# State space layer: scan inputs multiplied on GpSimd, one scan over both batches

## What is computed

```
xp = xi @ W_x
delta = softplus(xp[..., :1] @ W_dt.T + b_dt)
Bp = xp[..., 1:d_state + 1]
Cp = xp[..., d_state + 1:]
A = -exp(A_log)
def step(h, inp):
    x_t, dt, Bt, Ct = inp
    A_bar = exp(dt[..., None] * A)
    h = A_bar * h + dt[..., None] * Bt[:, None, :] * x_t[..., None]
    y_t = einsum('bds,bs->bd', h, Ct) + D * x_t
    return (h, y_t)
```

## Time and profile before

| what | value |
|---|---|
| median of 3 runs | 2915.17 us (2914.5 to 2917.82) |
| the profiled execution's own time | 2910.92 us |
| its span in the trace | 2909.1 us |
| PE busy | 2417.7 us, 83% |
| DVE busy | 1550.1 us, 53% |
| ACT busy | 1058.6 us, 36% |
| POOL busy | 284.9 us, 10% |
| the stage of the 64 units, from the first u to the last hc | 2028.3 to 2188.4 us |

### The profile page before, as it was taken

The page is one execution under the profiler, slowest core; times in us unless marked ns, Lnnn a source line. Parts: engine busy times, 40 slices in busy tenths (PEclk is TensorE's granted clock), DMA queues, the critical chain, the costliest instruction groups (busy, mean ns, idle before and its releaser), DMA issues. The chain is left out here.

```text
span 2909.1 us, 39020 instructions
## 1 busy us (share of the span) xinstructions
PE 2417.7 (83%) x15028; PEld 1411.4 (49%) x15032; DVE 1550.1 (53%) x2487; ACT 1058.6 (36%) x1954; POOL 284.9 (10%) x589
## 2 busy tenths in 40 slices
PE   2899999688996959999983996785787979788778
PEld 1344444345895634444441554251225837555447
DVE  3778777232221638888845874234996533232433
ACT  2466666321111315777751552122221223021310
POOL 0453000010000000000000550000000000010100
PEclk8899999887998978999996567886877989898879
DMA  8887553110553896555400000101002341110200
GB/s 218 195 189 165 95 94 51 46 46 6 217 229 145 270 238 126 123 95 120 69 12 28 12 1 31 51 1 56 4 0 87 116 193 54 51 41 0 95 1 8
DMA packets 108646, 260.20 MB, mean 89 GB/s; under 512 B 11942, under 2 KB 83302, under 8 KB 94310
## 3 DMA queue, kind: packets, MB, share of 16 engines
q1 hardware_dynamic: 103276, 210.17, 28.4%
q0 software_dynamic: 1584, 34.60, 3.0%
q10 hardware_dynamic: 3600, 12.91, 1.1%
HBM read 212.72 MB, written 44.92 MB: 89 GB/s over the span
## 5 line engine op out<-in xcount | busy, mean ns | idle before, releaser
L664 DVE TENSOR_REDUCE sta_parts<-sta_psA 128x1 f32<-128x1024 f32 x544 | 625.6, 1187 | 193.9 <-PE sta_psA L580 192.1
L722 ACT ACTIVATE sta_probs<-sta_psS 128x512 f32<-128x512 f32 x1056 | 575.8, 597 | 274.4 <-PE sta_psS L591 272.3
L591 PE MATMUL sta_psS<-L_xattn_qS,L_xattn_kst 99*128 99x256 bf16 x2112 | 356.1, 278 | 11.5 <-ACT sta_probs L722 6.6
L580 PE MATMUL sta_psA<-L_xattn_kst,L_xattn_qS 99*128 99x512 bf16 x1088 | 293.7, 388 | 52.5 <-PEq L59 37.9
L591 PEld LDWEIGHTS sta_psS<-L_xattn_qS,L_xattn_kst 99*128 99x128 bf16 x2112 | 161.3, 98 | 259.1 <-ACT sta_probs L722 183.4
L601 PE MATMUL sta_psO<-sta_probs,L_xattna_V 128*32 128x256 f32 x2560 | 189.5, 385 | 0.0
L580 PEld LDWEIGHTS sta_psA<-L_xattn_kst,L_xattn_qS 99*128 99x128 bf16 x1088 | 104.3, 99 | 137.6 <-DVE sta_parts L664 45.9
L202 ACT ACT_TABLE_LOAD x14 | 18.0, 1283 | 334.8 <-PEq L59 316.6
L2274 PE MATMUL l2t_psY<-l2t_hc,top_consts_weights 128*128 128x512 f32 x128 | 92.5, 839 | 31.6 <-DVE l2t_hc L2310 31.5
L601 PE MATMUL sta_psO<-sta_probs,L_xattn_V 128*32 128x256 f32 x1536 | 114.3, 388 | 0.0
L1006 ACT ACTIVATE sht_probs<-sht_psS 128x768 f32<-128x768 f32 (+1 forms) x64 | 55.3, 863 | 149.4 <-PE sht_psS L850 100.3
(11 more groups left out here) (614 smaller groups left out, 4048.5 us busy)
## 6 DMA issues: line engine op xcount, KB each, us to landing
L_xattn_kst<-L_xattn_keys SPq DMA_DIRECT2D x192, 136.0 KB
L_xattn_kst<-L_xattn_keys SPq DMA_DIRECT2D x192, 128.0 KB
L_xattn_values<-prj_rows SPq DMA_DIRECT2D x64, 256.0 KB, 3.8
L_xattn_keys<-prj_parts SPq DMA_DIRECT2D x32, 384.0 KB, 3.9
L_xattna_V<-in_ctxV SPq DMA_DIRECT2D x5, 2048.0 KB, 11.7
L_xattna_V<-L_xattn_values SPq DMA_DIRECT2D x5, 2048.0 KB, 11.3
l2f_W<-in_M SPq DMA_DIRECT2D x10, 1024.0 KB, 7.5
L_xattn_keys<-sta_bparts SPq DMA_DIRECT2D x24, 384.0 KB, 7.2
```

What stands on the lines that cost most here:

```text
L580: last = nc.tensor.matmul(psA[:, u % 2, col:col + rhs.shape[1]], lhsT, rhs, start=True, stop=True)
L591: last = nc.tensor.matmul(psS[:, at % 2, j * T:(j + 1) * T], lhsT, rhs, start=True, stop=True)
L664: nc.vector.tensor_reduce(into(parts[:, u // n % 2]), view(psA[:, u % 2, :]), AX.X, ALU.max).then_inc(max_taken, 1)
L722: nc.scalar.activation(probs[:, u % NP, i * 512:(i + 1) * 512], psS[:, at % 2, :], ACT.Exp, scale=scale).then_inc(probs_ready, 1)
```

## The change

The products `u` move from DVE to POOL (L2308 of the changed kernel). ACT first copies psB of a state from PSUM into a new SBUF tile `rowsB` with two buffers (L2289); POOL multiplies rowsB with dx, both in SBUF, into `u`, now a ring of 3. DVE runs one scan over all 512 tokens for each unit (L2320) in place of two. So that the second batch starts from zero, column 0 and column 256 of `decay` stay at zero: DVE clears the ring once (L2313), and ACT writes only steps 1 to 255 of each batch (L2298), in one instruction of 2 x 255 elements. PE also waits, before it overwrites a psB buffer, for the copy of what was in it.

```diff
@@ -2244,11 +2244,18 @@
             psC = p2.ps("psC", [P, 2, 512])
             psY = p2.ps("psY", [P, CH, 512])
             decay = p2.sb("decay", [P, 3, NTOK])
-            u = p2.sb("u", [P, 2, NTOK])
+            u = p2.sb("u", [P, 3, NTOK])
             h = p2.sb("h", [P, 2, NTOK])
             hc = p2.sb("hc", [P, 3, NTOK])
-            with stage(nc, "spread", "input_ready", "decay_ready", "states_ready", "read_ready", "summed", "dve_step", "ahead_loaded") as \
-                    (block, spread, input_ready, decay_ready, states_ready, read_ready, summed, dve_step, ahead_loaded):
+            rowsB = p2.sb("rowsB", [P, 2, NTOK])
+            with stage(nc, "spread", "rows_copied", "starts_cleared", "input_ready", "decay_ready", "states_ready", "read_ready", "summed", "dve_step",
+                       "ahead_loaded") as \
+                    (block, spread, rows_copied, starts_cleared, input_ready, decay_ready, states_ready, read_ready, summed, dve_step, ahead_loaded):
+
+                def after_first(x):
+
+                    return x.rearrange("p (b t) -> p b t", b=B)[:, :, 1:T]
+
                 @block.sync
                 def _(sp):
                     load_ahead(sp, ahead, ahead_loaded)
@@ -2257,7 +2264,7 @@
                 def _(pe):
                     def spread_rows(s):
                         if s >= 2:
-
+                            pe.wait_ge(rows_copied, s - 1)
                             pe.wait_ge(read_ready, (s - 1) * CH)
                         n = 2 * NS + 1
                         for ps, r in ((psB, 1 + s), (psC, 1 + NS + s)):
@@ -2275,36 +2282,43 @@
 
                 @block.scalar
                 def _(act):
+                    def copy_rows(s):
+                        act.wait_ge(spread, s + 1)
+                        if s >= 2:
+                            act.wait_ge(input_ready, (s - 1) * CH)
+                        nc.scalar.copy(rowsB[:, s % 2, :], psB[:, s % 2, :]).then_inc(rows_copied, 1)
+
+                    copy_rows(0)
+                    act.wait_ge(starts_cleared, 1)
                     for i in range(NS * CH):
+                        if i % CH == 1 and i // CH + 1 < NS:
+                            copy_rows(i // CH + 1)
                         if i >= 3:
-                            act.wait_ge(states_ready, 2 * (i - 2))
-                        nc.scalar.activation(decay[:, i % 3, :], delta[:, i % CH, :], ACT.Exp, scale=A[:, i // CH:i // CH + 1]).then_inc(decay_ready, 1)
+                            act.wait_ge(states_ready, i - 2)
+                        nc.scalar.activation(after_first(decay[:, i % 3, :]), after_first(delta[:, i % CH, :]), ACT.Exp,
+                                             scale=A[:, i // CH:i // CH + 1]).then_inc(decay_ready, 1)
+
+                @block.gpsimd
+                def _(gp):
+                    for i in range(NS * CH):
+                        s, m = i // CH, i % CH
+                        gp.wait_ge(rows_copied, s + 1)
+                        if i >= 3:
+                            gp.wait_ge(states_ready, i - 2)
+                        nc.gpsimd.tensor_tensor(u[:, i % 3, :], rowsB[:, s % 2, :], dx[:, m, :], ALU.mult).then_inc(input_ready, 1)
 
                 @block.vector
                 def _(dve):
                     N = NS * CH
-
-                    def inputs(i):
-                        s, m = i // CH, i % CH
-                        dve.wait_ge(spread, s + 1)
-                        if i >= 2:
-
-                            dve.wait_ge(states_ready, 2 * (i - 1))
-                        nc.vector.tensor_tensor(u[:, i % 2, :], psB[:, s % 2, :], dx[:, m, :], ALU.mult).then_inc(input_ready, 1)
-
-                    inputs(0)
+                    nc.vector.memset(decay[:], 0.0).then_inc(starts_cleared, 1)
                     for i in range(N):
                         s, m = i // CH, i % CH
-                        if i + 1 < N:
-                            inputs(i + 1)
                         dve.wait_ge(decay_ready, i + 1)
                         dve.wait_ge(input_ready, i + 1)
                         if i >= 2:
                             dve.wait_ge(read_ready, i - 1)
-                        for b in range(B):
-                            c = slice(b * T, (b + 1) * T)
-                            nc.vector.tensor_tensor_scan(h[:, i % 2, c], decay[:, i % 3, c], u[:, i % 2, c], 0.0, ALU.mult, ALU.add).then_inc(states_ready, 1)
-                        dve.wait_ge(states_ready, 2 * (i + 1))
+                        nc.vector.tensor_tensor_scan(h[:, i % 2, :], decay[:, i % 3, :], u[:, i % 3, :], 0.0, ALU.mult, ALU.add).then_inc(states_ready, 1)
+                        dve.wait_ge(states_ready, i + 1)
                         if i >= 3:
                             dve.wait_ge(summed, i - 2)
                         nc.vector.tensor_tensor(hc[:, i % 3, :], psC[:, s % 2, :], h[:, i % 2, :], ALU.mult).then_inc(read_ready, 1)
```

## The result

The changed kernel takes 2945.11 us (median of 4 runs, 2943.23 to 2946.82) against 2915.0 for the kernel before (4 runs, 2914.5 to 2917.82): a ratio of 1.0101, 95% interval 1.0084 to 1.0119, slower by 30 us. The profiled execution took 2944.77 us, its span is 2942.9 us, against 2910.92 and 2909.1. POOL's time grew by the 85 us of its 64 products. The first scan starts at 2030.63 and the last hc at 2222.80, where the earlier trace rows had 2187.70: nearly all of the difference lies in the stage of the 64 units. PE's granted clock over that stage is 0.68, where the earlier trace rows had 0.77.

A forecast was written before the change was run, and what follows sets the result against it. DVE was taken to bound the stage, at 2.50 us a unit. Fourteen states at the expected clock mix, plus start and end, gave 139.5 + 44.8 - 140.0 = +44 us, so 2959 us; range 2925 to 2978.

The forecast's parts named there:

- DVE's own work: On DVE, u leaves and one scan replaces two: a unit with all inputs there takes 1.85 us, 0.65 less.
- The wait on ACT: On ACT, the next state's copy waits for PE's spread and holds back the exps and DVE's scans, in 14 states.
- X: Time from T to the start of scan 4s + 1: 4.38 us at PE's high clock, 7.12 at the low.
- The port: At SBUF, POOL's product goes first and DVE's scan waits: a contended unit takes 2.45 us, bounds 2.35 and 2.57.
- The fourth rival: At SBUF, POOL two products ahead takes its turn after the scan: 2.20 us a unit, +36 us; chance within the forecast's 0.67.
- The start and the end: Outside the 14 waiting states: scan 1 starts at 2032.9, and the last hc starts 7.91 us after the last T.
- First T: T is the end of unit 4s - 1's hc, from which a state is counted; the first was put at 2039.8.
- The clock: On PE, 10 of 14 spreads at the low clock (state 13.95 us), 4 at the high (11.21 us).
- Rival 1: No conflict between DVE's scan and POOL's product: 1.85 us a unit, +25 us with the expected clock mix; chance 0.20.
- rival 2: Conflict at SBUF, but PE stays at the high clock: +17 us; chance 0.10.
- rival 3: Faster: no conflict, high clock, and a spread reaching ACT sooner; a chain 0.5 us shorter gives -9 us; chance 0.03.
- signs named for a right forecast: DVE idle once a state, 1.9 or 4.7 us; scans 1.2 or 1.8; hc 0.69; stage 44 us longer; clock below 0.77.

The follow-up runs named there:

- either release of POOL: POOL's product i released by the scan of unit i - 3 or by its hc, in the changed kernel with its copy moved back: 2887.55 and 2889.95 us.
- the late copy: Changed kernel with ACT's copy of the next state's rows behind the exp of unit 4s + 3, not ahead of unit 4s + 1's: 2887.55 us.
- kernel with PE kept busy: Changed kernel with the products of units 4s + 1 and 4s + 2 made twice on PE, 32 more in all: 2945.58 us.
- pair with added products: Kernel before plus 64 POOL products into a tile nobody reads, released by the unit's scans or by its hc: 2911.98 and 2956.52 us.
- two different kernels: Changed kernel with POOL released by hc instead of the scan, 2946.47 us, and changed kernel with 32 products made twice on PE, 2945.58 us.

## Why the prediction was right, and by how much it was off

The direction, the mechanism and the order of size were right: 2959 predicted, 2945.1 measured, inside the range. Going through its steps:

- **DVE's own work.** 1.21 for the scan, 1.85 for a free unit: measured 1.215 and 1.86. Right.
- **The wait on ACT.** X = 4.38 and 7.12: measured 4.37 and 7.12. The terms as they are written add up to 4.40 and 7.15, so that it fits to 0.01 is partly luck. It was read from PE's timeline of the kernel before without a row of the operation itself. Moving the copy takes the wait away and the loss with it, with either release of POOL, so it is shown and not only read.
- **The port.** 2.45 a unit: measured 2.49 in states 1 to 14. The scan is issued 0.49 after POOL's product and blocked for 0.63, so POOL keeps it off for 1.12 us from its own start, where I had 0.07 + 1.07; the hand-over to POOL is 0.15, where I had 0.10. The Trainium skill's rule in full length, 2.57, overshoots: the blocked scan gets going 0.14 before POOL's record ends. POOL's lead of three, gained while DVE waits, was right too: the late copy takes it away and the unit falls to 2.14.
- **The fourth rival**, turns with a shorter lead, I had priced at 2.20 and as an alternative. It is real, 2.14, and holds in the first state; then POOL gets ahead in the first wait.
- **The start and the end.** First T at 2039.8 predicted, 2039.4 measured; the last hc 7.91 behind the last T predicted, 8.01 measured.
- **The clock: the term that was mis-sized.** "I expect 10 of the 14 spreads at the low clock and 4 at the high." Measured: 5 low (state 14.0 us), 5 high (11.3), and 4 with a low product and a high spread (12.2), which sum to 175.4 us where I had 184.3. I had reckoned with strings of products without a gap as what mostly lifts the clock. The trace shows it rising also where two or three products at the low clock, 2.07 us in every 2.49, had gone ahead, and falling again where they stood at 1.1 in 2.49 or PE had waited 2.2 us, in a pattern that repeats every three states. The kernel with PE kept busy moved the waits by 9.5 us, which shows how much of the stage hangs on this term.

From +44 to +30: the clock is 9 us of the difference, and the stretch behind the stage was 1.3 shorter. The remaining 3.7 is the median's, for which I had added 4.3: the profiled execution of the kernel before lay 4 us below the median of its runs, that of the changed kernel at its own.

Rival 1, no conflict at the port, is refuted by the blocked scans and by the pair with added products; rival 2, a clock that stays high, by the 5 low spreads; rival 3, which needed both, fell with them. Of the signs named for a right forecast, all came but the sizes of two: the stage is 34 us longer and not 44, and a third length of wait appeared.

## What to carry to other kernels

A product moved to an idle engine is free only if its operands do not go through what the busy engine needs: with two SBUF operands on each side, DVE and POOL work one after the other, and a PSUM operand on DVE's side sets them free (1.86 us a unit instead of 2.14 or 2.49). Before adding a copy to an engine that feeds the bottleneck, look at what is queued behind it and how late its input comes; here three exps further back in ACT's program were worth 57 us. And where two engines take turns, the one that may run ahead will use its lead at the worst moment, so look at what releases it as well as at what it needs; here that was worth 9 us of the stage, which did not reach the kernel's time.

## What was not expected of the hardware

- The same two loops, scan on DVE and product on POOL, have two steady beats, 2.14 and 2.49 us, and with the same release of POOL which one holds depends on how far ahead POOL was when the last stall ended.
- 9 us won in one stage did not reach the whole time, in two different kernels. Their traces show 729.0 and 729.5 us behind the last hc against 720.1, with unchanged code at a granted clock of 0.94 instead of 1.00 in one stretch; the cause is open. A gain of a third of a per cent in a stage whose end moves should be checked on the whole kernel.
- Reading decay from PSUM made the scan no slower: 1.215 us in either memory.
